# Two layer normalisations' subtract and multiply on GpSimd, with new orders on all engines

## The reference

```python
# layer 0: graph attention
h = x @ W_fc.T;  f1 = h @ a1;  f2 = h @ a2
scores = leaky_relu(f1[:, :, None] + f2[:, None, :], 0.2)
scores = where(adj == 0, -1e9, scores)
h_prime = softmax(scores, axis=2) @ x
x = layernorm(x + elu(h_prime))
# layer 1: similarity
xn = x / sqrt(max(sum(x * x), 1e-12))
out = ((xn @ xn.T) @ adj) @ x
x = layernorm(x + out)
# layernorm(x) = (x - mean) / sqrt(var + 1e-5)
```

## Time and profile before

| what | value |
|---|---|
| median of 3 runs | 348.49 us (347.63 to 349.29) |
| profiled execution, its own time | 350.04 us |
| span in that profile, first to last instruction | 348.2 us |
| busy: TensorE, ScalarE, VectorE, GpSimd | 90%, 85%, 81%, 61% |
| mean granted TensorE clock | 0.983 of full |

### The profile page before, as it was taken

One profiled execution on the slowest core, in us unless ns is written; L12 is line 12 of the kernel. 1 busy time (PEld: TensorE's weight loads), 2 busy tenths in 40 slices (PEclk: granted clock), 3 DMA queues, 4 the chain that ended last, 5 costly groups with the idle time before them and its releaser, 6 DMA issues.

```text
span 348.2 us, 7246 instructions
## 1 busy us (share of the span) xinstructions
PE 311.9 (90%) x2372; PEld 297.4 (85%) x2372; DVE 281.1 (81%) x996; ACT 295.4 (85%) x609; POOL 212.2 (61%) x231
## 2 busy tenths in 40 slices
PE   3076699999999999999999999999999999997880
PEld 1065699999999999999999999999999999996860
DVE  3278988989898989899898989898989988766231
ACT  1399797999999999999999999999999999945242
POOL 3212757685967676666668596767666677655301
PEclk9999999999999999999999999999999999999697
DMA  6961044255464464553634545446355252101011
GB/s 199 287 182 36 27 123 121 60 161 144 122 180 124 128 175 125 142 161 72 188 107 162 142 122 174 128 126 180 121 132 172 73 171 62 56 7 60 2 60 60
DMA packets 33972, 42.43 MB, mean 122 GB/s; under 512 B 1136, under 2 KB 25744, under 8 KB 33936
## 3 DMA queue, kind: packets, MB, share of 16 engines
q0 software_dynamic: 16896, 25.17, 26.5%
q1 hardware_dynamic: 17040, 16.81, 15.5%
HBM read 33.59 MB, written 8.39 MB: 121 GB/s over the span
## 4 chain that ended last, share of the span: by engine, by line
PE 80%; POOL 6%; issue 5%; DMA 4%; DVE 2%; ACT 1%; SPq 0%; ACTq 0%; POOLq 0%; DVEq 0%
PE ps_l L711 15%; PE ps_l L673 9%; PE ps_l L674 9%; PE ps_h L643 8%; PE ps_h L644 8%; PE ps_h L645 8%; PE ps_probT L627 7%; PE ps_l L697 4%; PE ps_l L699 4%; PE ps_l L698 4%; PE ps_l L683 4%; DMA x_hi<-x 3%; PE ps_f L616 2%; POOL y L228 1%; POOL x_lo L221 1%
## 5 line engine op out<-in xcount | busy, mean ns | idle before, releaser
L643 PE MATMUL ps_h<-x_hi,probT_hi 128*128 128x256 f32 x256 | 78.4, 306 | 3.1 <-ACT y L517 2.1
L644 PE MATMUL ps_h<-x_lo,probT_hi 128*128 128x256 f32 x256 | 71.5, 279 | 0.0
L645 PE MATMUL ps_h<-x_hi,probT_lo 128*128 128x256 f32 x256 | 71.4, 279 | 0.0
L673 PE MATMUL ps_l<-xn_hi,adj_sb 128*128 128x256 f32 x256 | 66.3, 295 | 3.1 <-POOL xn_lo L261 3.1
L674 PE MATMUL ps_l<-xn_lo,adj_sb 128*128 128x256 f32 x256 | 64.8, 289 | 0.0
L711 PE MATMUL ps_l<-w_sb,xnT 128*128 128x256 f32 x256 | 62.9, 380 | 0.3
L261 POOL TENSOR_TENSOR xn_lo<-xn,xn_hi 128x1024 fp32r<-128x1024 f32 x16 | 38.5, 2404 | 37.1 <-ACT xn_hi L525 37.1
L643 PEld LDWEIGHTS ps_h<-x_hi,probT_hi 128*128 128x128 f32 x256 | 48.2, 188 | 7.1 <-DVE probT_lo L363 3.3
L673 PEld LDWEIGHTS ps_l<-xn_hi,adj_sb 128*128 128x128 f32 x256 | 50.8, 198 | 3.9 <-issue 3.5
L627 PE MATMUL ps_probT<-ident,prob 128*128 128x128 f32 x256 | 39.4, 278 | 13.6 <-ACT prob L491 12.9
L674 PEld LDWEIGHTS ps_l<-xn_lo,adj_sb 128*128 128x128 f32 x256 | 50.8, 198 | 0.0
(11 more groups left out here) (57 smaller groups left out, 775.0 us busy)
## 6 DMA issues: line engine op xcount, KB each, us to landing
adj_sb<-adj POOLq DMA_DIRECT2D x16, 1024.0 KB, 6.0
x_sb<-x SPq DMA_DIRECT2D x16, 512.0 KB, 4.6
x_hi<-x POOLq DMA_DIRECT2D x16, 512.0 KB, 4.0
out<-o_sb SPq DMA_DIRECT2D x16, 512.0 KB, 3.1
attn_cols<-w_attn SPq DMA_DIRECT2D x2, 0.1 KB, 1.6
wfc<-w_fc SPq DMA_DIRECT2D x1, 32.0 KB, 1.7
```

What stands on the lines that cost most here:

```text
L643: nc.tensor.matmul(ps, probT_hi[:, c, blk], x_hi[n][:, k, :], start=(k == 0), stop=False)
L644: nc.tensor.matmul(ps, probT_hi[:, c, blk], x_lo[n][:, k, :], start=False, stop=False)
L645: last = nc.tensor.matmul(ps, probT_lo[:, c, blk], x_hi[n][:, k, :], start=False, stop=(k == NC - 1))
L673: nc.tensor.matmul(ps, a, xn_hi[n][:, k, :], start=(k == 0), stop=False)
```

## The change

`normalise` moves from VectorE to GpSimd with the same arithmetic: four instructions with two per-partition scalars. `normalise2` moves from ScalarE to GpSimd and becomes subtract and multiply too, so the small instructions that made minus the mean (`neg_mean2`) and the shift (`shift2`, `bias2`) go. As buffers are now read by other engines, four waits are added: `normalise` waits for y2_ok of three graphs before, `row_moments` and `elu_exp` for xn_ok of three graphs before, `residual2` for o_ok of three graphs before; the wait for the stored output moves to GpSimd. The bodies of the loops on GpSimd, VectorE, ScalarE and TensorE get new orders, and the boundaries of a step are drawn elsewhere (graph numbers in them differ by one). SyncE's list stays.

```diff
+            def normalise(g):
+                pool.wait_ge(powers_ok, g + 1)
+                if graph(g - NBUF):
+                    pool.wait_ge(y2_ok, NC * (g - NBUF + 1))
+                for c in range(NC):
+                    last = pool.tensor_scalar(xn[n][:, c, :], y[n][:, c, :], mv[n][:, c, 0:1], powers[n][:, 1, c:c + 1],
+                                              ALU.subtract, ALU.mult)
+                last.then_inc(xn_ok, 1)
...
-                pool.tensor_scalar(neg_mean2[n][:], mv2[n][:, :, 0], -1.0, None, ALU.mult).then_inc(ve2_ok, 1)
...
-            def shift2(g):
...
+            def normalise2(g):
+                pool.wait_ge(scale2_ok, g + 1)
+                if graph(g - 1):
+                    pool.wait_ge(out_stored, 16 * g)
+                for c in range(NC):
+                    last = pool.tensor_scalar(o_sb[:, c, :], y2[n][:, c, :], mv2[n][:, c, 0:1], scale2[n][:, c:c + 1],
+                                              ALU.subtract, ALU.mult)
+                last.then_inc(o_ok, 1)
```

More of the change, by code:

```diff
@@ L245, in power @@
                 pool.tensor_tensor(powers[n][:], moments[n][:], minus_half[:], ALU.pow).then_inc(powers_ok, 1)
+            def normalise(g):
+                if not graph(g):
+                    return
+                n = g % NBUF
+                pool.wait_ge(powers_ok, g + 1)
[5 more added lines that the diff above has]
+                last.then_inc(xn_ok, 1)
             def norm(g):
@@ L274, in power2 @@
                 n = g % NBUF
-                pool.wait_ge(ve2_ok, 2 * (g + 1))
+                pool.wait_ge(ve2_ok, g + 1)
                 pool.tensor_tensor(scale2[n][:], ve2[n][:], minus_half[:, 0:NC], ALU.pow).then_inc(scale2_ok, 1)
-            def shift2(g):
+            def normalise2(g):
                 if not graph(g):
@@ L282, in shift2 @@
                 pool.wait_ge(scale2_ok, g + 1)
-                pool.tensor_tensor(bias2[n][:], scale2[n][:], neg_mean2[n][:], ALU.mult).then_inc(norm2_ok, 1)
-            for i in STEPS:
-                norm(i)
-                split_xn(i)
-                load_x_hi(i + 2)
[L289 to L296, removed]
+                if graph(g - 1):
[4 more added lines that the diff above has]
+                last.then_inc(o_ok, 1)
+            for i in STEPS:
+                normalise(i - 1)
+                shifted_moments2(i - 3)
+                power2(i - 3)
+                split_xn(i - 1)
+                norm(i - 1)
+                normalise2(i - 3)
+                residual_sum(i)
+                load_adj(i + 2)
+                split_x(i + 1)
+                shifted_moments(i)
+                load_x_hi(i + 2)
+                power(i)
         @block.vector
@@ L380, in row_moments @@
                     dve.wait_ge(mv_ok, g)
+                if graph(g - NBUF):
+                    dve.wait_ge(xn_ok, g - NBUF + 1)
                 for c in range(NC):
@@ L387, in row_moments @@
                 last.then_inc(mv_ok, 1)
[L389 to L397, removed]
             def z_lo_part(g, c):
@@ L414, in residual2 @@
                     dve.wait_ge(nrm_ok, g + 1)
+                    if graph(g - NBUF):
+                        dve.wait_ge(o_ok, g - NBUF + 1)
                 nc.vector.scalar_tensor_tensor(out=y2[n][:, c, :], in0=xn[n][:, c, :], scalar=nrm[n][:, c:c + 1],
@@ L510, in elu_exp @@
                         act.wait_ge(y_ok, g)
+                    if graph(g - NBUF):
+                        act.wait_ge(xn_ok, g - NBUF + 1)
                 nc.scalar.activation(exp_h[:, c, :], ps_h[c % 2][:, 0:D], ACT.Exp, scale=rden[n][:, c:c + 1])
@@ L551, in copy_w @@
                 nc.scalar.activation(w_sb[:, d, :], ps_l1[(W0 + d) % 3][:, 0:D], ACT.Copy).then_inc(w_ok, 1)
-            def normalise2(g):
-                if not graph(g):
-                    return
-                n = g % NBUF
-                act.wait_ge(norm2_ok, g + 1)
-                if graph(g - 1):
-                    act.wait_ge(out_stored, 16 * g)
-                for c in range(NC):
-                    last = nc.scalar.activation(o_sb[:, c, :], y2[n][:, c, :], ACT.Identity,
-                                                bias=bias2[n][:, c:c + 1], scale=scale2[n][:, c:c + 1])
-                last.then_inc(o_ok, 1)
```

143 lines of the change are left out of this document (69 added, 74 removed).

## The result

The kernel after takes 427.16 us (median; 426.84 to 427.71), the kernel before 348.06 on the same chip (347.54 to 349.29): a ratio of 1.2268, 95% interval 1.223 to 1.2306. The profiled execution took 427.13 us for a span of 425.3. The prediction, 347.2 us with a range to 361, was wrong in sign and far outside its range.

The account below looks back on a forecast made before the run. TensorE was taken to bound the step (18.86 us), with GpSimd's added work hidden. Order -0.4, head 0, end -1.0 and stalls +0.1 made -1.3 us, so 347.2 us; range 344.5 to 361.

Parts of the forecast that it names:

- t: Length of one new 128x256 subtract-and-multiply on GpSimd, eight a step: taken as 0.45 us, between 0.40 and 0.79.
- The upper bound: Highest length allowed for the new GpSimd instruction: 0.79 us, from the 2.15 ns an element of two-input TENSOR_TENSOR.
- step from AFFINE_SELECT: Lower estimate of the new GpSimd instruction from a one-input 128x128 one of 0.28 us: 0.40 us.
- Rival 1: GpSimd becomes the bound of the step, with 361 us at t = 0.60 and some 380 at 0.79; chance 0.28.
- 13.5 + 8t: GpSimd's work in a step, us: its other work plus eight new instructions; 17.1 of the 18.8 expected.
- The loop of 14.8 + 8t: Residual, GpSimd's whole chain, then the next residual, never side by side: 18.4 us a step, 18.8 at t = 0.50.
- The orders: TensorE's new order in the steady step: 0.03 us gained a step, bounds 0 and 0.1, 0.4 us over 14 steps.
- Head: Time until the first z: 45.0 against 45.06 us, so 0 change, bounds -1.5 and +1.5.
- Rival 3: The head keeps the 2.5 us that an earlier residual_sum(0) wins: 344.7 us; chance 0.10.
- End: After attention of graph 15: reordering and a shorter last normalisation (-0.8) together give -1.0 us.
- rival 2: GpSimd fits, but its collisions with node_scores and residual cost TensorE some 0.3 us a step: 351.6 us; chance 0.12.

Follow-up runs that it names:

- gpsimd_forms: Separate kernel without the network: GpSimd instruction forms timed at 256 and 1024 columns, alone and beside VectorE subtractions; one execution, 96.37 us.
- edges: Kernel before, with residual_sum of graphs 0 and 15, split_xn of 15 and three chunks of the last normalise2 moved to VectorE: 343.9 us, ratio 0.9874.
- the doses: Kernel after with the eight normalising GpSimd instructions cut from 256 to 64 or 8 columns, rest zero: 359.47 and 349.22 us.
- eight_columns: Kernel after with each normalising GpSimd instruction cut to 8 of 256 columns, rest zero: 349.22 us, ratio 1.0038.
- only_second: Kernel after with normalise back on VectorE ahead of probT_lo(i,2), only normalise2 on GpSimd: 391.82 us, ratio 1.1248.
- undo_placed: Kernel after with normalise on VectorE ahead of probT_lo(i,2) and normalise2 on ScalarE in pieces, last behind the next scale_z(i-2,3): 445.73 us, ratio 1.279.
- undo_chunk_earlier: As undo_placed, but the last chunk of ScalarE's normalise2 moved forward to stand behind elu_relu(i,3): 390.39 us, ratio 1.1192.

## Why the prediction was wrong, by its own steps

**The step that failed is t.** The prediction put the unseen instruction between 0.40 and 0.79 us and took 0.45. It is 1.22 alone (gpsimd_forms) and 1.33 in the kernel. The upper bound had been worked out from TENSOR_TENSOR's slope, in the belief that two tensor inputs are the dearest form. The prediction's step from AFFINE_SELECT on 128x128 in 0.28 us to this instruction had no ground but "one tensor input". Which form of instruction it is decides, not how many tensors it reads: the slope is 2.1 ns an element for two tensors, 2.5 for one scalar operation and 3.3 for two; a whole instruction of 1024 columns comes to 1.0 ns an element for a copy and 1.8 with a repeated operand.

The Trainium skill (GPSIMD Engine Reference, section "Engine selection") has one-input elementwise work at "roughly line-rate" on GpSimd. The copy's 1.0 ns an element agrees with that; 2.5 and 3.3 do not, and the measurement decides. Its other half, that two-input work takes twice VectorE's time, fits edges' 1.23 against 2.35.

**Rival 1 had the mechanism.** GpSimd's need, 13.5 + 8t, holds: with t as measured, 24.1 against 23.79 seen, and the doses follow it. 15 steps of +4.58 make 68.8 of the 77.1 us. Its chance was 0.28; what kept it from more, and its times within 380, was the false bound of t.

**The loop of 14.8 + 8t was wrong by its 1.3 us.** It rested on "residual never runs beside a large GpSimd instruction", from one collision with L261, which has two tensor inputs. In the kernel after:

```profile
191.25 1.22 DVE L385 SCALAR_TENSOR_TENSOR exp_h<-exp_h,x_sb 128x1024 f32<-128x1024 f32 x1
...
199.46 0.89 DVE L360 SCALAR_TENSOR_TENSOR neg_z<-row_max,f 128x2 f32<-128x2 f32 x1
```

Residual ran at full pace within L294 (189.36 to 194.76), while negate_max was held to the end of x_lo (197.95 + 2.37 = 200.32). The Trainium skill (SBUF — State Buffer, section "Who interferes with whom") says that a VectorE instruction with two SBUF inputs contends with a GpSimd one that reads SBUF, and calls contention an exclusive lock. Beside two-tensor instructions the traces agree; beside subtract and multiply with scalars they don't: the mean of 420 became 463 ns. So by the sum t decides at 0.67, not at 0.50.

**The orders.** Predicted +0.03 us a step of gain, found 0.00 (18.85 against 18.86, eight_columns); the 0.4 us was too small to matter. What the prediction didn't see is that these orders are worth 43 us when GpSimd is the bound, against the one placement in the old orders that was tried.

**Head.** Predicted 0 with bounds of 1.5; it is +5.7. On GpSimd normalise(0) starts 1.5 us later (41.61 against 40.06 on VectorE before) and lasts 5.31 instead of 1.38, which makes 5.5 of it. Two errors of the prediction are in that. One is t: four times t is 5.3 instead of 1.8. The other is that residual_sum(0) was to come at 30.1 and came at 32.61, as before: residual stands behind masked_f2 in VectorE's new list, and that waited for its mask until 29.69. With 4t = 1.8 the same sum would still be +2.0 (an estimate), outside the bounds. The +3.0 of eight_columns has something else in it. There xn is complete at 42.83, but ScalarE starts xn_hi only at 44.43, behind work that waits for TensorE at a clock of 0.50; the prediction had no term for the clock. Rival 3, which would keep the 2.5, falls as residual_sum(0) came no earlier.

**End.** Predicted -1.0. The orders give -3.5 (eight_columns, with its short t), and at full t it is +2.6: behind z of graph 15, GpSimd has the last normalise2 of graph 14 (4.8 us), then that of graph 15, which waits for the store of 14:

```profile
409.16 4.84 POOL L294 TENSOR_SCALAR o_sb<-y,mv,scale 128x256 f32<-128x256 f32 x4
...
417.15 4.83 POOL L294 TENSOR_SCALAR o_sb<-y,mv,scale 128x256 f32<-128x256 f32 x4 [0.47 <-DMA out<-o_sb]
```

**Collisions (rival 2)** didn't set the step of the kernel after: negate_max is held there, as shown, but GpSimd has no gap to lose. They decided the placements: a node_scores was held for 2.2 us a step in only_second, undo_placed and undo_chunk_earlier. The four new waits and the moved loads were hidden, as predicted, until a placement made the store late.

**What stays open.** No undoing of the move in the new orders came back to 348 us: the best is 363.96, with a step of 20.0. Whether these orders have any place for the two normalisations on VectorE and ScalarE that leaves TensorE full wasn't found. Why GpSimd takes longer for an operation with a scalar or a constant on one tensor than for one on two tensors isn't shown either, nor how much TensorE's clock has in the 43 us and in the head.

## What to carry to other kernels

A form of instruction that the trace doesn't show has no upper bound from its neighbours: before moving work to another engine, measure that instruction at its size there, and if that can't be done, let the chance of "far above" stay. Then compare the sum of the engine's list with the step of the engine that bounds; here an error of 0.88 us in t came eight times a step, in 16 steps. Look at the ends too, where a slow engine stands on the chain alone: there 1.3% was to be had by moving work the other way, from GpSimd to VectorE.
